# Another prologue for a fused attention and convolution kernel: plain f32 mixing, Wq in pieces, o of the first unit copied by TensorE, projections six units ahead

## The reference

```python
att = softmax(gelu(gelu(c @ W0 + b0) @ W1 + b1) @ W2 + b2)          # [64, 8]
y   = einsum('bk,koi->boi', att, weight) @ x + (att @ bias_k)[:, :, None]
q, k, v = y @ Wq + bq, y @ Wk + bk, y @ Wv + bv
o   = softmax(outer(q, k) / sqrt(32)) @ v
x   = x + broadcast(o)
u   = conv1d(x, conv_w, groups=4, pad=4) + (c @ ctx_w)[:, :, None] + bias
x   = x + u @ (scale * (nibbles(packed) - zero_point)).T + ffn_bias
```

## Time and profile before

| | |
|---|---|
| median of 3 runs | 493.93 us (493.15 to 495.46) |
| profiled execution | 494.59 us |
| its span, first to last instruction | 492.8 us |
| TensorE busy | 450.7 us, 91% |
| VectorE, ScalarE, GpSimd busy | 333.2, 228.3, 346.8 us |
| mean granted TensorE clock | 0.971 of full |
| DMA | 79.78 MB, engines busy 49.7% |

### The profile page before, as it was taken

One profiled execution on the slowest core, in us unless ns is written; L12 is line 12 of the kernel. 1 busy time (PEld: TensorE's weight loads), 2 busy tenths in 40 slices (PEclk: granted clock), 3 DMA queues, 4 the chain that ended last, 5 costly groups with the idle time before them and its releaser, 6 DMA issues. The chain is left out here.

```text
span 492.8 us, 7038 instructions
## 1 busy us (share of the span) xinstructions
PE 450.7 (91%) x2403; PEld 373.5 (76%) x2403; DVE 333.2 (68%) x532; ACT 228.3 (46%) x458; POOL 346.8 (70%) x329
## 2 busy tenths in 40 slices
PE   3998272999999999999999999999999999997996
PEld 2998151777877888888888888787888888775885
DVE  4639685739793968677785949495968678692121
ACT  2705570546354545545463645454544535472520
POOL 2400493969697968797696969697869788696920
PEclk9999596799999999999999999999999999999999
DMA  8956324254555556473827464546547352606112
GB/s 338 413 212 217 106 89 108 65 132 184 139 224 142 221 133 235 116 252 97 269 97 214 149 171 161 150 175 163 200 116 252 106 178 93 190 4 189 47 44 85
DMA packets 55522, 79.78 MB, mean 162 GB/s; under 512 B 41904, under 2 KB 41904, under 8 KB 50864
## 3 DMA queue, kind: packets, MB, share of 16 engines
q1 hardware_dynamic: 55472, 79.08, 49.7%
HBM read 61.76 MB, written 17.30 MB: 160 GB/s over the span
## 5 line engine op out<-in xcount | busy, mean ns | idle before, releaser
L725 PE MATMUL p_f<-w_ffn,u_lo 128*128 128x512 f32 x512 | 204.1, 399 | 0.0
L725 PE MATMUL p_f<-w_ffn,u_hi 128*128 128x512 f32 x512 | 202.2, 405 | 1.1 <-DVE u_lo L605 1.1
L419 ACT ACTIVATE u_sb<-p_conv,u_bias,cols_sb 128x128 f32<-128x128 f32 x256 | 96.2, 457 | 59.9 <-PE p_conv L709 59.0
L327 POOL TENSOR_TENSOR xc<-xc,o_c 128x384 f32<-128x384 f32 x64 | 56.7, 886 | 92.2 <-DMA o_c<-o_dram 90.8
L725 PEld LDWEIGHTS p_f<-w_ffn,u_hi 128*128 128x128 f32 x512 | 97.0, 189 | 21.2 <-issue 1.3
L725 PEld LDWEIGHTS p_f<-w_ffn,u_lo 128*128 128x128 f32 x512 | 97.1, 190 | 18.3
L613 DVE TENSOR_TENSOR xn<-p_f,xn 128x512 f32<-128x512 f32 x64 | 44.0, 688 | 84.5 <-PE p_f L725 84.5
L336 POOL TENSOR_TENSOR c_lo<-xc,c_hi 128x516 fp32r<-128x516 f32 x60 | 78.3, 1310 | 9.7 <-issue 6.2
L410 ACT ACTIVATE c_hi<-xc 128x516 fp32r<-128x516 f32 x64 | 40.8, 638 | 87.6 <-POOL xc L330 87.5
L349 POOL TENSOR_TENSOR xn<-xn,bias_n 128x1024 f32<-128x1024 f32 x32 | 77.1, 2408 | 2.5
L709 PE MATMUL p_conv<-c_hi,cw_hi 128*128 128x512 f32 x128 | 53.6, 419 | 26.0 <-POOL c_lo L336 14.6
(11 more groups left out here) (99 smaller groups left out, 502.5 us busy)
## 6 DMA issues: line engine op xcount, KB each, us to landing
xc<-xc_in_in SPq DMA_DIRECT2D x16, 1032.0 KB, 5.0
xt<-xt_in_in SPq DMA_DIRECT2D x16, 1024.0 KB, 7.6
xn<-xn_in_in SPq DMA_DIRECT2D x16, 1024.0 KB, 6.0
out<-xn SPq DMA_DIRECT2D x32, 512.0 KB, 6.5
o_c<-o_dram SPq DMA_DIRECT2D x128, 32.0 KB, 2.1
xn<-wq_in SPq DMA_DIRECT2D x3, 1024.0 KB, 10.6
xt<-wq_in SPq DMA_DIRECT2D x1, 1024.0 KB, 6.5
prob<-mix_w_in SPq DMA_DIRECT2D x1, 512.0 KB, 4.4
```

The costliest lines, as they stand in the source:

```text
L327: eng.tensor_tensor(x4[:, :, :, 0:3], x4[:, :, :, 0:3], o.unsqueeze(3).broadcast_to([P, UB, DH, 3]), ALU.add).then_inc(s_add, 1)
L419: ins = eng.activation(u_sb[:, g % 2, n * P:(n + 1) * P], p_conv[g % 2][:, n * P:(n + 1) * P], ACT.Identity, bias=u_bias[:, g, UB * b + n: ...
L725: return mm(p_f[half][:, :], u[:, d % 2, r, t * P:(t + 1) * P], w_ffn[:, r, 512 * half:512 * half + 512], **flags)
```

## The change

Parts, in the order in which they act.

1. Mixing weights in plain f32: the rounding into parts, the third part and GpSimd's copy go; the matrices are laid out in 32 rows (four slices of eight), `own` masks the slice, and 32 f32 products of 128 columns with 64 output rows take the place of 64. Four copies to `mix_t` take the place of 16. Seven f32 products of `ones` (`keep_busy`) follow on TensorE.
2. Wq in five pieces (2, 2, 2, 1, 1 row blocks) at other places of the load order; VectorE sums each when it is there, GpSimd halves one block. The column sums are interleaved with unit 0's projection. `mix_w` is loaded on ScalarE's queue. The weights of the linear layer are converted in four quarters, three on ScalarE, one on GpSimd; the bias of u moves from VectorE to ScalarE.
3. o is stored as 128 values a token (each of 32 four times), `o_dram` and `o_c` are four times as large, and one GpSimd add takes the place of three for each group. GpSimd adds the bias before o in the residual.
4. Unit 0 is worked in two tiles (p = 0 and 1) from the add on: `copy_o` on TensorE selects and shifts o into PSUM, in the layout of the convolution, `add_first` on VectorE adds it from there. `linear` of tile 0 starts before conv of tile 1.
5. `project` runs six units ahead (z for seven units is kept) and not three; the prologue projects up to unit 6.

```diff
-            eng.wait_ge(s_mwr, 1)
-            eng.wait_ge(s_mwd, 1)
-            for m in range(8):
-                rows = slice(32 * (m // 2), 32 * (m // 2) + 3 * KE)
-                if m >= 4:
-                    eng.wait_ge(s_mixt, 2 * (m - 3))
-                for n in range(8):
-                    s = 8 * (m % 2) + n
-                    last = mm(p_mixed[m % 4][:, B * n:B * n + B], mixw_r[rows, s, :, :].rearrange("k h i -> k (h i)"),
-                              att_t[rows, :], start=True, stop=True)
-                last.then_inc(s_mixed, 1)
+            for n in range(4):
+                for j in range(4):
+                    rows = slice(32 * j, 32 * j + 32)
+                    for h in range(2):
+                        last = mm(p_mixed[j][h * S:h * S + S, P * n:P * n + P].rearrange("p (s t) -> p s t", s=4), mixw[rows, n, :], att_t[rows, :, h::2],
+                                  start=True, stop=True)
+                    if n == 3:
+                        last.then_inc(s_mixed, 1)
...
+            keep_busy(p_conv[0], 7)
...
             for r in range(R):
-                if r % 2 == 0:
-                    eng.wait_ge(s_w3[r // 2], 1)
+                eng.wait_ge(s_w3, r + 1)
+                last = mm(col3(1), ones[:, :], w3[:, r, :], start=(r == 0), stop=(r == R - 1))
...
+            def copy_o(p, g):
...
+                for n in range(TN):
+                    for h in range(2):
+                        last = mm(copies(p, g)[h * S:h * S + S, n, :], sel[:, n * G + g, 4 * h:4 * h + 4, :].rearrange("p r c -> p (r c)"),
+                                  o_sb[:, 0, p, h:h + MW], start=True, stop=True)
+                last.then_inc(s_rep, 1)
...
+            for g in range(G):
+                copy_o(0, g)
+            conv(0, 0)
+            conv(0, 1)
+            project(3, 0, 0)
+            transpose_u(0, 0)
+            conv(0, 2)
+            copy_o(1, 0)
+            copy_o(1, 1)
+            transpose_u(0, 1)
+            conv(0, 3)
+            transpose_u(0, 2)
+            copy_o(1, 2)
+            transpose_u(0, 3)
+            copy_o(1, 3)
+            project(3, 0, 1)
+            for slot in range(SLOTS // 2):
+                linear(0, slot)
...
+                if slot == 1:
+                    conv(1, 0)
...
+            for slot in range(SLOTS // 2):
+                linear(1, slot)
+                if slot == 0:
+                    mix(2)
+            project(5, 0)
+            project(5, 1)
+            project(6, 0)
+            conv(2, 0)
...
+            mix(3)
+            for d in range(1, NU):
                 for slot in range(SLOTS):
...
+                    if d + 6 < NU and slot in Z_SLOT:
+                        project(d + 6, Z_SLOT.index(slot))
+                    if d + 3 < NU and slot == MIX_SLOT:
+                        mix(d + 3)
```

On GpSimd, in every unit from the second on:

```diff
-                eng.tensor_tensor(x4[:, :, :, 0:3], x4[:, :, :, 0:3], o.unsqueeze(3).broadcast_to([P, UB, DH, 3]), ALU.add).then_inc(s_add, 1)
-                eng.tensor_tensor(x4[0:64, :, :, 3], x4[0:64, :, :, 3], o[0:64], ALU.add).then_inc(s_add, 1)
-                eng.wait_ge(s_add, 3 * (G * b + g) + 1)
-                eng.tensor_tensor(x0[64:P, :, :, 0], x0[64:P, :, :, 0], o[64:P], ALU.add).then_inc(s_add, 1)
+                x = rows_of(xc[:, u % 2, :, :, :], p, g)
+                eng.tensor_tensor(x, x, rows_of(o_c, p, g), ALU.add).then_inc(s_add, 1)
```

On VectorE, between unit 0 and the first full loop:

```diff
             scores(0)
             attend(0, 0)
+            sum_exp(0, 1)
+            add_first(0, 0)
+            add_first(0, 1)
+            times_v(0, 1)
+            add_first(0, 2)
+            add_first(0, 3)
+            sum_v(0, 1)
+            divide(0, 1)
+            softmax_top(1)
...
+            finish(1, 1)
+            sum_exp(2, 0)
+            times_v(2, 0)
+            c_low(TU, 0)
+            sum_v(2, 0)
+            c_low(TU, 1)
+            divide(2, 0)
+            sum_exp(2, 1)
+            c_low(TU, 2)
+            times_v(2, 1)
+            c_low(TU, 3)
```

More of the change, by code:

```diff
@@ L451, in _ @@
             u_high(0, 3)
[L452 to L477 removed]
+            convert_weights(1, 1)
@@ new lines, in _ @@
+            c_high(1, 0)
+            c_high(1, 1)
+            exp(1, 0)
+            c_high(1, 2)
+            c_high(1, 3)
+            z_copy(3)
+            u_copy(1, 0)
+            u_copy(1, 1)
+            u_high(1, 0)
+            u_copy(1, 2)
+            exp(1, 1)
+            u_high(1, 1)
+            u_copy(1, 3)
+            u_high(1, 2)
+            u_high(1, 3)
+            z_copy(4)
+            exp(2, 0)
+            exp(2, 1)
+            z_copy(5)
+            for p in range(TU, NP):
+                b = unit_of(p)
+                a = b + 1
+                c_high(p, 0)
+                c_high(p, 1)
+                if b > 1 and a < NU:
+                    exp(a, 0)
+                c_high(p, 2)
+                if b == 1:
+                    c_high(p, 3)
+                u_copy(p, 0)
+                if b > 1 and a < NU:
+                    exp(a, 1)
+                if b > 1:
+                    c_high(p, 3)
+                u_copy(p, 1)
+                if 1 < b < NU - 5:
+                    z_copy(b + 5)
+                u_high(p, 0)
+                u_copy(p, 2)
+                u_high(p, 1)
+                if b == 1:
+                    z_copy(6)
+                u_copy(p, 3)
+                u_high(p, 2)
+                u_high(p, 3)
@@ L650, in _ @@
+            u_low(1, 3)
+            sum_exp(1, 1)
+            finish(0, 1)
+            times_v(1, 1)
             sum_v(1, 1)
             divide(1, 1)
-            for i in range(2, NI):
+            softmax_top(2)
+            finish(1, 0)
+            score(2, 0)
+            subtract(2, 0)
+            score(2, 1)
+            subtract(2, 1)
+            finish(1, 1)
[4 more added lines that the diff above has]
+            c_low(TU, 1)
@@ L795, in _ @@
             last.then_inc(s_z, 1)
-            eng.wait_ge(s_b3, 1)
-            for r in range(R):
-                last = mm(col3(1), ones[:, :], w3[:, r, :], start=(r == 0), stop=(r == R - 1))
-            last.then_inc(s_col, 1)
             eng.wait_ge(s_colc, 1)
-            eng.wait_ge(s_mixb, 2)
-            eng.wait_ge(s_mixt, 16)
+            eng.wait_ge(s_mixt, 4)
             mix(0)
+            project(1, 0)
+            project(1, 1)
             eng.wait_ge(s_ctx, 16)
```

762 lines of the change are left out of this document (418 added, 344 removed).

## The result

The changed kernel takes 517.99 us (median of 4 runs, 516.06 to 521.78) against 494.15 (493.15 to 495.46) for the kernel before: ratio 1.049, 95% interval 1.0426 to 1.0555. It is slower by 24 us where I forecast 21.3 faster. The profiled execution has a span of 516.0 us and a mean granted clock of 0.957. In all that follows a ratio is to the kernel before, run in the same session, and leaves out executions over 1.5% slower than the fastest of the same kernel; medians and ranges hold them.

What follows compares the result with a forecast made beforehand. TensorE's work plus its holes in the prologue and near the end was taken to bound the kernel. Terms -14.1 (unit 1's loop earlier), -7.2 (projections) and 0 (tail) sum to -21.3: 493.9 to 472.6 us, range 465 to 486.

Steps and rivals of the forecast that it cites:

- First and second step: Prologue: k_sb of unit 0 at 25.2 us instead of 32.53, then first linear product at 47.5 instead of 72.70.
- mixing in series: Rival, weight mixing in the prologue: records run one behind the other, +8.4 us on everything behind, 481 us; chance 0.13.
- Wq lands in time: Prologue input loads: 4.7 MB ahead of Wq's last piece at 434 GB/s is 11 us after first arrival near 3.
- Third step: First linear to first full loop: unit 1's loop starts at 94.8 us with handoffs, 14.1 early; two more projections done, 7.2.
- slow third part: Rival, before unit 1's loop: VectorE's order slower than laid out, TensorE's idle there doubled, 479 to 484 us; chance 0.10.
- Fourth step: Loops: conv's inputs 2.2 us spare, later stalls about what the one hole costs now, wider spreads nothing; 0, bounds -1.4 and +2.8.
- My own formula: Spreads landing d us late cost d in the prologue, (d-2.2)/2 in nine loops, d/2 in five: 8d-9.9.
- The turning point of 3.9 us: Landing delay d of the wide spreads from which its price, 8d-9.9, passes the 21.3 us gain.
- Both rivals with a late landing: Wide spreads of o: landing 2.5 us later, 483 us, chance 0.12; or moving at 59 GB/s, 535 us, chance 0.07.
- spreads by bytes: Rival, spreads of o: 1 MB at 59 GB/s takes 17 us, d near 9, +62, so 535 us; chance 0.07.
- The price of the projections: Two more projections done before unit 1's loop, up to 6 instead of 4: 2 x 3.6 = 7.2 us saved.

Runs made afterwards that it cites:

- narrow form: Changed kernel with o of unit 1 and later stored, spread and added as before (32 values a token, three GpSimd adds a group): 478.92 us, ratio 0.972.

## Why the prediction was wrong

**First and second step, to the first linear product: right in time, by luck in part.** k_sb is 0.3 us late, the first product 0.1 us off. But within the first step two terms are wrong and cancel. The mixing takes 2.0 us (9.58 to 11.6) and not 5.2: its 64 records run beside each other, 0.03 us apart, where 0.213 was the pace of one behind another. With att_t 0.5 us later than I took, it ends 2.5 us before my 14.1. The rival "mixing in series" is out. Then the 48 records of unit 0's projection and column sums take 8.6 us (15.37 to 23.95) and not 6.1:

```profile
15.91 1.06 PE L946 MATMUL p_conv<-w,xt 128*128 128x96 f32 x4
...
17.19 1.06 PE L946 MATMUL p_conv<-w,xt 128*128 128x96 f32 x4
...
22.00 0.61 PE L946 MATMUL p_conv<-w,xt 128*128 128x96 f32 x4
...
22.67 0.61 PE L946 MATMUL p_conv<-w,xt 128*128 128x96 f32 x4
```

Six records are 1.28 us (0.213 each) up to about 21 and 0.67 (0.11 each) from then on, so some thirty go at the slow pace where I took eight. The granted clock is 1.00 in both stretches; what sets the pace stays open. "Wq lands in time" was nearly so: VectorE waits for it until 17.89, 1.1 us, and TensorE does not. (My two sums there, 14.1 + 9.1 and 14.1 + 8.4 + 0.7, give 23.2 and not 23.4.)

**Third step: two misses.** "7.9 through DRAM as in rows 3 makes 76.1": in the changed kernel 16.5 us (68.12 to 84.6). With the narrow spreads it is 76.08, to the tenth. The other, "conv ends at 90.8 and unit 1's loop starts at 92.6": ScalarE's order, which I had not followed through, made it 98.5 in the narrow form (92.94 with the order changed), and behind it stood unit 2's landing, which I had not looked at (with both changed unit 1's last `finish` is at 122.28). The rival "slow third part" had the size right (479 to 484; the narrow form takes 478.9), and the reason wrong: it put VectorE's order at fault. These 5.5 us at unit 1's last `finish` are most of the 6.3 us between 472.6 and the narrow form.

**Fourth step: this is where it failed.** The step puts the later landing of the wide spreads at nothing: "Each unit now sends 128 KB instead of 32 KB per spread ... so they had room; wide loads go at 434. I add nothing, with 3 us as the upper bound." The runs show the delay in its place. Over the narrow form it was 8.7 us in the prologue (16.5 against the narrow form's 7.8) and 6.4 in the last loop (13.7 against 7.3). My own formula (d for the prologue, (d - 2.2)/2 and d/2 for the loops) with these two is 8.7 + 9 x (6.4 - 2.2)/2 + 5 x 6.4/2 = 43.6 us; measured are 39.1. In the two traces it comes as 12.9 us up to unit 1's last `finish` (139.58 against 126.72), 14.8 in the next nine loops (27.75 against 26.10 each), 11.5 in the last five (122.93 against 111.45):

```profile
139.58 0.69 DVE L707 TENSOR_TENSOR xn<-p_f,xn 128x512 f32<-128x512 f32 x1 [2.12 <-PE p_f L870]
...
389.33 0.69 DVE L707 TENSOR_TENSOR xn<-p_f,xn 128x512 f32<-128x512 f32 x1 [2.13 <-PE p_f L870]
...
512.26 0.69 DVE L707 TENSOR_TENSOR xn<-p_f,xn 128x512 f32<-128x512 f32 x1 [2.71 <-PE p_f L870]
```

```profile
126.72 0.69 DVE L721 TENSOR_TENSOR xn<-p_f,xn 128x512 f32<-128x512 f32 x1 [2.12 <-PE p_f L884]
...
361.64 0.69 DVE L721 TENSOR_TENSOR xn<-p_f,xn 128x512 f32<-128x512 f32 x1 [2.13 <-PE p_f L884]
...
473.09 0.69 DVE L721 TENSOR_TENSOR xn<-p_f,xn 128x512 f32<-128x512 f32 x1 [2.71 <-PE p_f L884]
```

So how a delay turns into time was right in outline, and its size and its chance were wrong. The turning point of 3.9 us was not tested by a run. The parts of the formula are 8.7, 18.9 and 16.0, so its sum is nearer to the measured one than its parts are. Both rivals with a late landing named this path; "spreads by bytes", which had 0.07, was right that bytes count, and took them at 17 us a unit where 12.2 were measured. The row that would have told it is the earlier trace rows, read another way. I took the share of 0.43 as room. But 59 GB/s at a share of 0.43 is 137 GB/s at full share, where the input loads move 434 at 1.03: the small spreads already kept the engines three times as long for their bytes. By an estimate from these, 1 MB at 137 GB/s is 7.7 us, 5.8 more than 256 KB, above the turning point. That row could not tell whether the price was one for packets (which then stay as many) or for bytes into few places; the first would have cost nothing, the second this. Such a fork deserves an even chance. Of the Trainium skill I weighed "DMA: Bandwidth & Descriptors" (512 B enough for line rate, table at its top), and not "SBUF — State Buffer" (Door 1), which speaks against this change. Here the same 512 B packets took 12.2 us for 1 MB into 16 neighbours and 7.4 into 128 partitions: their size alone does not give the rate.

**The price of the projections** (-7.2 for two) was not tested by itself: the run with one fewer lost 7 to 9 us, a part of it by the late store of o. The five loops without a projection take 24.2 us each in the narrow form (337.81 to 458.58), where I had 22.9 and about 3.3 of stalls in all, so 23.6 each. In the whole, the narrow form gained 14.5 to 15 us of the 21.3.

## What to carry to other kernels

Before a transfer is widened, divide the GB/s of a stretch by its DMA share: a low share at a low rate is not room. Look at where the destination lies too: here 1 MB in transfers of 16 neighbouring partitions took 12.2 us where 7.4 did for all 128. Follow a gain to the next wait: here unit 1's first linear product came 5.6 us earlier and the end stayed, for the next unit's o came no sooner. In a queue, what is issued just ahead of a small store that many wait for is part of that store's time: with a 1 MB load ahead it took 3.3 us instead of 1.4, with a load and eight spreads 5.7 instead of 1.5, with the spreads alone 2.3. And a change of when a buffer comes free moves a load in the queue, as the run with one projection fewer shows.

## What the runs showed of the hardware, unexpected

1 MB in transfers of 16 partitions takes 12.2 us into neighbours and 7.8 into partitions four apart. A DMA share of 1.16 stands beside 180 GB/s, and one of 1.03 beside 434: a full share says nothing of the rate. f32 products on 32 rows and 64 columns of the array each took 2.0 us for 64 records, where one behind another at 0.213 us would be 13.6. Early in the kernel f32 records of one shape follow 0.213 us apart, and from about 21 us on 0.11, at a granted clock of 1.00 in both. Four issues on ScalarE's queue took 3 us of its own time. And a hole of 4.5 us on TensorE is followed by four us at 0.50, while waits of 0.3 to 0.9 us in the ten us ahead of it left the clock at 1.00.
